# A two-layer decoder on one core: the last stage's units ahead of its later key scores, and the value biases of two stages carried into the output biases

## What is computed

```python
x = x + L0_attn(ln(x))          # random-feature attention, 16 heads of 8, biases on q, k, v, o
x = x + L0_xattn(ln(x), ctx)    # softmax attention over the context, masked by query row, biases
x = x + L0_ffn(ln(x))           # four binary trees that route each row to a leaf of a table
x = x + L1_attn(ln(x))          # causal softmax attention, no biases
x = x + L1_xattn(ln(x), ctx)    # softmax attention over the context, bias on o
x = x + L1_ffn(ln(x))           # product keys: 8 heads, top 16 of 32 x 32 experts
```

```python
v = split_heads(x @ Wv.T + bv)
out = einsum(qf, context, d_inv)        # rows are averages: the weights of a row sum to 1
return out @ Wo.T + bo

sx, ix = top_k(sim[0], 16); sy, iy = top_k(sim[1], 16)     # sim: scores of xn against the keys
scores, pk = top_k(sx[:, None] + sy[None, :], 16)
h = gelu(xn @ table_down[indices].T) * softmax(scores)
out = h @ table_up[indices]
```

## Time and profile before

| | us |
|---|---|
| median of 3 runs | 779.19 (779.06, 779.19, 783.67) |
| the profiled execution | 782.85 |
| its span | 781.1 |
| PE busy | 658.5 (84%) |
| DVE busy | 605.9 (78%) |
| ACT busy | 442.2 (57%) |
| POOL busy | 320.4 (41%) |

### The profile page before, as it was taken

The page is one execution under the profiler, slowest core; times in us unless marked ns, Lnnn a source line. Parts: engine busy times, 40 slices in busy tenths (PEclk is TensorE's granted clock), DMA queues, the critical chain, the costliest instruction groups (busy, mean ns, idle before and its releaser), DMA issues. The chain is left out here.

```text
span 781.1 us, 14578 instructions
## 1 busy us (share of the span) xinstructions
PE 658.5 (84%) x4849; PEld 500.8 (64%) x4849; DVE 605.9 (78%) x2444; ACT 442.2 (57%) x1064; POOL 320.4 (41%) x315
## 2 busy tenths in 40 slices
PE   4969978786888989898788799989879688888898
PEld 2538534443476877786777467655446677787897
DVE  5794686874788989996879777877547689999984
ACT  1333105554565988798977255566545655555562
POOL 4150242821424333231146322221013698888983
PEclk9995558988987999999999999999989899999999
DMA  8000021100786989998652221111000000000000
GB/s 251 3 1 3 12 73 47 43 2 3 297 373 236 422 306 381 340 418 353 224 218 52 61 63 48 48 45 46 2 1 1 1 1 5 4 5 5 4 5 8
DMA packets 38931, 86.07 MB, mean 110 GB/s; under 512 B 3993, under 2 KB 30146, under 8 KB 30664
## 3 DMA queue, kind: packets, MB, share of 16 engines
q0 software_dynamic: 9216, 69.47, 22.6%
q1 hardware_dynamic: 29640, 15.67, 7.6%
HBM read 74.43 MB, written 0.52 MB: 96 GB/s over the span
## 5 line engine op out<-in xcount | busy, mean ns | idle before, releaser
L842 ACT ACTIVATE arena<-arena,hact 128x128 f32<-128x128 f32 x512 | 155.4, 388 | 1.0
L722 ACT ACTIVATE arena<-psum 128x512 f32<-128x512 f32 (+1 forms) x192 | 101.5, 561 | 57.6 <-PE psum L1475 57.1
L617 POOL TENSOR_TENSOR arena<-arena 128x1024 f32<-128x1024 f32 x64 | 121.1, 1911 | 22.6 <-DVE arena L1317 17.0
L1170 DVE CUSTOM_DVE_ANT_0 arena<-arena,fx 128x128 f32<-128x128 f32 x384 | 106.3, 345 | 5.4 <-DMA arena<-tab_q,leaf_no 3.4
L888 ACT ACTIVATE psum<-arena,tneg 128x1024 f32<-128x1024 f32 x64 | 71.5, 1118 | 62.2 <-DVE arena L1317 29.6
L1863 PE MATMUL psum<-arena 128*128 128x128 f32 x688 | 86.7, 283 | 20.3 <-DVE arena L1317 12.9
L976 DVE TENSOR_REDUCE rowmax<-psum 128x2 f32<-128x512 f32 x128 | 81.5, 686 | 24.1 <-PE psum L1457 22.1
L1863 PEld LDWEIGHTS psum<-arena 128*128 128x128 f32 x688 | 82.0, 197 | 23.8 <-DVE arena L1317 15.4
L1754 PE MATMUL psum<-identf,arena 128*128 128x128 f32 x544 | 77.2, 299 | 5.5 <-ACT arena L842 4.4
L1457 PE MATMUL psum<-arena 128*128 128x256 bf16 (+1 forms) x384 | 73.8, 283 | 9.3 <-DVE rowmax L976 8.2
L1754 PE MATMUL psum<-arena,identf 128*128 128x128 f32 x544 | 73.4, 285 | 6.0 <-ACT arena L842 5.4
(11 more groups left out here) (235 smaller groups left out, 1197.0 us busy)
## 6 DMA issues: line engine op xcount, KB each, us to landing
arena<-parts SPq DMA_DIRECT2D x144, 64.0 KB
w_sb<-attn_w SPq DMA_DIRECT2D x1, 768.0 KB, 8.2
x<-x_in SPq DMA_DIRECT2D x1, 512.0 KB, 4.4
fx<-ctx_in SPq DMA_DIRECT2D x1, 512.0 KB, 5.0
picked<-mask_in SPq DMA_DIRECT2D x1, 512.0 KB, 6.1
wq_sb<-peer_wq SPq DMA_DIRECT2D x1, 512.0 KB, 7.9
down_sb<-table_down SPq DMA_DIRECT2D x1, 512.0 KB, 8.9
up_sb<-table_up SPq DMA_DIRECT2D x1, 512.0 KB, 8.8
```

The lines of the kernel that those rows point to most:

```text
L617: nc.gpsimd.tensor_tensor(grid[k % 3].rearrange("p (i j) -> p i j", i=PK), sim[:, t, h, :].unsqueeze(2).to_broadcast([P, PK, PK]), sim[:, ...
L722: nc.scalar.activation(probs[k % (2 * HG)][:, 0:w], bank(2 + k % 2, 0, w), ACT.Exp, scale=float(D) ** -0.5).then_inc(probs_ready, 1)
L842: a = nc.scalar.activation(w, w, ACT.Copy, scale=hact[i % 2][:, l:l + 1])
L1170: i = nc.vector.tensor_tensor_reduce(w, w, src, 1.0, r[:, LW * E + l:LW * E + l + 1], ALU.mult, ALU.add, hid[g % 4][:, l:l + 1])
```

## The change

**In the last stage.** PE no longer does the key scores 4 to 7 ahead of the units of the second half. It does `sims(4)` and `sims(5)` behind the last unit, and `sims(6)` and `sims(7)` behind the mix of heads 0 and 1 of tile 0. ACT copies score 4 ahead of the tile loop and scores 5, 6 and 7 behind the exponentials of heads 1, 2 and 3. Scores 4 to 7 use banks 2 and 3 (`sim_bank`), so PE waits for all of them ahead of tile 1. ACT makes the diagonals of tile 0 in pairs behind the first four exponentials, where it made all behind the second. DVE sums the weights of tile 0 ahead of the first product, where it did so behind it.

```diff
+        def out_bias(a):
+            return psum[0:3, 7 * BANK + P * (a + 1):7 * BANK + P * (a + 2)]
...
+        def sim_bank(t):
+            return bank(t % 2 + t // 4 * 2)
...
@@ POOL @@
+            power(0)
             link(nc.gpsimd.memset(blockm[:, :, :], 1.0))
...
             for n in range(B):
-                power(n)
+                if n:
+                    power(n)
                 squares(n)
...
@@ ACT @@
-            copy(bias_c[:, 4:6], bank(6, 4, 6), columns_ready)
+            copy(bias_c[:, 2:9], bank(6, 2, 9), columns_ready)
...
             def peer():
-                for i in range(2):
-                    if i:
-                        evac_px(i)
-                    for t in range(2 if i == 0 else 4, 4 + 4 * i):
-                        evac_sims(t)
-                    for u in range(B * i, B * i + B):
-                        evac_unit(u)
+                evac_sims(2)
+                evac_sims(3)
+                for u in range(B):
+                    evac_unit(u)
+                evac_px(1)
+                for u in range(B, UNITS):
+                    evac_unit(u)
+                evac_sims(4)
                 act.wait_ge(unit_ready, UNITS)
...
-                        if k == 1:
-                            for i in range(4):
-                                diagonals(0, 2 * i, 2 * i + 2)
+                        if k < 4:
+                            diagonals(0, 2 * k, 2 * k + 2)
+                        if 1 <= k < 4:
+                            evac_sims(4 + k)
...
@@ DVE @@
-            split_bias(nc.vector, link, 2 * P, 4 * P)
-            nc.vector.tensor_copy(bias_w[:, 0:1], bias_p[:, 2 * P:2 * P + 1]).then_inc(bias_ready, 1)
...
+                if 0 < n < B - 1:
+                    o = bias_sb[:, (4 * n - 1) * P:4 * n * P]
+                    link(nc.vector.tensor_tensor(o, out_bias(n - 1), o, ALU.add))
                 link(nc.vector.tensor_copy(sv, half_norm[:, 1, :]))
...
                 if 0 < n < B - 1:
-                    split_bias(nc.vector, link, (4 + 2 * n) * P, min(6 + 2 * n, 9) * P)
+                    o = (4 * n - 1) * P
+                    split_bias(nc.vector, link, o, o + n * P)
...
+                weight_sum(0)
                 for t in range(T):
...
-                        if k == 0:
-                            weight_sum(0)
...
@@ PE @@
-            BIAS = {(0, 2): 2, (0, 3): 3, (1, 2): 6, (1, 3): 7, (3, 3): 8}
+            BIAS = {(0, 3): 3, (1, 3): 7, (3, 3): 8}
...
-            pe.wait_ge(bias_ready, 1)
             pre_v(0)
...
+                if 1 <= n < B - 1:
+                    value_bias(n - 1)
...
+            def value_bias(a):
+                if a == 0:
+                    pe.wait_ge(columns_ready, 1)
+                else:
+                    pe.wait_ge(in_ctx, 48)
+                nc.tensor.matmul(out_bias(a), bias_c[:, 4 * a + 2:4 * a + 3].to_broadcast([P, 3]), w_sb[:, 4 * a + 3, :],
+                                 start=True, stop=True)
...
+                sims(2)
+                sims(3)
+                for u in range(B):
+                    unit(u)
+                turn_px(1)
+                for u in range(B, UNITS):
+                    unit(u)
+                sims(4)
+                sims(5)
                 pe.wait_ge(unit_ready, UNITS)
-                pe.wait_ge(sim_ready, T)
+                pe.wait_ge(sim_ready, 4)
...
                 for t in range(T):
+                    if t == 1:
+                        pe.wait_ge(sim_ready, T)
...
+                        if t == 0 and h in (0, 1):
+                            sims(6 + h)
```

33 lines of the change are left out of this document (13 added, 20 removed).

## The result

The changed kernel took 772.83 us (median of 769.13, 772.49, 773.16 and 773.53) against 779.42 for the kernel before in the same series, a ratio of 0.9893 with a 95% interval of 0.9847 to 0.994. That is 6.6 us, where the forecast was 2.9. Two further series of the changed kernel are among the experiments; the median of all its 15 executions is 771.3.

A forecast was written before the change was run, and what follows sets the result against it. It took as bounds DVE's 5.98 us wait for ACT's first exponential in the last stage, and DVE's nearly unbroken work in the opening. Opening -0.1 and last stage -2.8 took 779.19 to 776.3 us, range 771.5 to 780.9.

The forecast's parts named there:

- Last stage, -2.8: Tile 0: first exponential 2.35 us sooner, DVE's weight sum (0.43) moved into its wait; next choice 2.8 us sooner.
- The beat: Last stage's ring of waits between DVE, POOL and ACT, repeated each tile; claimed to carry 2.8 us to the end.
- rival E: Last stage: the ring's beat, not its start, sets the end; only 0.1 us is left, 779.1; chance 0.03.
- Rival B: Last stage, tile 0: PE at half clock makes tile 7's key score late; 2.1 us lost, 778.4; chance 0.11.
- the place with least room: Last stage, tile 0: the fifth exponential, behind tile 7's key score; claimed hidden with 0.6 us to spare.
- Opening, second pass, +1.34: DVE's second bias split, widened from 128 to 256 columns, its scaling held by POOL's clear; ends 1.34 us later.
- rival A: Opening: the second split pass is not held more than now, giving 1.3 us more, 775.0; chance 0.12.
- Opening, -0.95: PE's features start 0.95 us sooner: 0.65 from the first value projection, 0.3 from the earlier power on POOL.
- In the second stage the missing bias matmuls fall ... nothing: Second stage: they fall behind the projection POOL waits for, or on a PE waiting for DMA; worth nothing.
- Rival D: The half-clock stretch of PE containing 64 to 82 us ends early; 5.6 us won, 770.7; chance 0.12.
- one of my own signs of being wrong: Forecast is wrong if the half-clock stretch in which 64 to 82 us lie has another length.
- Rival C: Slower than before, if the half-clock stretch lasts some 3 us longer in dense work; 780.8; chance 0.10.

The follow-up runs named there:

- e11: Changed kernel plus 24 unread PE products in the gap behind the opening, and POOL's node split waiting for DVE's third five-operation chain: 763.94 us, ratio 0.9793.
- e1: Kernel before with only the last stage's part of the change: 777.17 us, ratio 0.9969.
- e16: Changed kernel as it is, measured again: 771.01 us, ratio 0.9876.
- e13: Changed kernel with PE's gap filled and POOL's node split in two, three operations early and eight behind DVE's third chain: 761.01 us, ratio 0.9767.
- e4: Kernel before with only the value biases carried into the output biases: 772.37 us, ratio 0.9899.
- e9: Changed kernel with POOL's node split waiting until DVE's third chain of five operations is done: 769.93 us, ratio 0.9855.
- e14: Kernel before with PE's gap filled and POOL's node split waiting behind DVE's third chain: 769.96 us, ratio 0.9867.
- e15: Changed kernel with an overwritten 3x128 product put back ahead of each second-stage value product: 775.43 us, ratio 0.9947.
- e8: Kernel before with only the second stage's value bias carried into its output bias: 773.28 us, ratio 0.9916.

## Where the prediction held and where it failed

- **Last stage, -2.8: right in mechanism, 0.3 to 0.9 too large.** Counted from the addition to `x` ahead of the stage (588.66 and 577.90, 10.76 apart), the first exponential is 2.04 sooner (612.96 and 600.16) where I had 2.35. The load starts 0.35 behind POOL's differences (598.65 against 597.90 + 0.40), and I had put it 0.06 behind. With `weight_sum`'s 0.43 this makes 2.48, and the stretch shows 2.5. But only the changed kernel's first profile and e11's have a tile 0 of 58.8; in the seven others with this last stage it takes 59.2 to 59.4, which is 1.9 to 2.1 less than 61.3. The beat carried the head start to the end (131.1 and 130.7), so rival E is out.
- **Rival B's mechanism is the usual case.** In those seven profiles PE does key score 6 at the lower speed (two matmuls 1.91 where they take 1.02, at a granted clock of 0.50 in e1 and e16), and ACT stands idle 2.72 ahead of its copy. In e1:

```profile
610.49 1.91 PE L1835 MATMUL psum<-wq_sb,maskrow 128*128 128x512 f32 x2
```

```profile
612.44 0.60 ACT L663 ACTIVATE arena<-psum 128x512 f32<-128x512 f32 x1 [2.72 <-PE psum L1835]
```

  DVE then waits 0.28 or 0.29 for ACT at the fourth product, so the place with least room lay one head ahead of where I had it, at score 6 and not at score 7. The cost is 0.6 and not 2.1. In the changed kernel's first profile the same idle is 1.54, and nothing is lost.
- **Opening, second pass, +1.34: wrong in the changed kernel's first profile, right in others.** The scaling was not held. It started at 42.54, POOL's clear at 42.75, and it took 0.28; the clear had been 0.13 ahead in my estimate. The pass takes 8.45 against 8.19. That is rival A. I gave it 0.12 although 0.13 us decided it, and behind an opening that had changed by microseconds that margin was worth nothing. Of ten profiles with the new pass seven show 8.45. In the other three it takes 9.5 to 9.6, about what I forecast: in e13 the scaling is held as I had it, in e4 and e9 one cast is held through both clears. The rows of e13 and of e9:

```profile
42.67 3.51 DVE L271 TENSOR_SCALAR bias_p<-arena,identf 3x256 bf16<-3x256 bf16 x1
```

```profile
43.25 6.58 DVE L274 CAST arena<-arena 3x256 bf16<-3x256 f32 x1
```

- **Opening, -0.95: too small, because I moved PE's instructions and left their speed.** The features start 1.39 sooner, and PE reaches full speed at 15.2 us. In e1, whose opening is the old code, it is 19.0 and round 3 starts at 52.32; before's profiled execution (24.1, 54.72) was a late one, as e14's was (54.56). So of the 4.0 us by which round 3 is sooner, some 2.4 are that execution's, and about 1.6 the change's. Over the other profiles of the changed opening the 1.6 scatters: round 3 starts anywhere from 49.85 to 51.76.
- **"In the second stage the missing bias matmuls fall ... nothing": this is the step that failed.** They are eight products, 2.0 us of PE, and they are on the path: in the first pair of profiles the stretches up to the first, the second and the third chain are each 0.5 to 0.9 shorter. The last 0.5 of it, the wait of 1.79 that becomes 1.28, decides how many of the third chain's operations are held. In the place of nothing, this term measured 4.4 us (e15 against e16, 12 and 7 executions), through the third chain and through the clock near 90 us and behind the chain. Nothing in the prediction stood for it, neither a term nor a rival, for I never read 147 to 160 us.
- **Rival D, the half-clock stretch: partly.** In the change it is over for good at 117.6 and not at 123.1, and it is broken from 90.3 to 97.1: 61.5 us at the lower level where it was 68.3. So one of my own signs of being wrong came, another length of this stretch. The 5.6 us that I gave D had no row behind it. The stretch from the first addition to the third unit is 2.0 shorter. It takes 64.8 to 66.2 in the unfilled kernels with the second stage's products and 63.5 to 64.9 in those without, and in e8, with the old opening, it is 64.9 against e1's 66.2, so this too hangs on those products and not on the opening alone. How much of it is the products' own time and how much the clock is not separated.
- **Rival C, a longer half-clock stretch,** did not come.

The forecast of -2.9 was then -2.8 that gave 1.9 to 2.5, and -0.1 that stood for about 1.6 (opening), 2.0 (first addition to third unit) and 2.5 to 4.6 (third unit: 24.1 less 21.6 or 19.5). These add up to 8.0 to 10.7, more than the 6.6 measured at first and about the 7.3 to 10.0 of the later series. They are differences of single profiled executions, so they bear the scatter named above.

Left open: what sets the moment at which PE reaches full speed in the opening (13.3 to 15.2 us in executions of the changed kernel, 18.6 to 24.1 in kernels with the old opening), why the clock comes back near 90 us where the second stage's products are gone, and why the stretch from 220 to 589 us differs by up to 7 us between executions whose code there is the same.

## What to carry to other kernels

Where DVE runs a chain of short operations on the path, look at what POOL does at that time: an operation of 0.2 us becomes one of 2 us, and half a microsecond of shift elsewhere decides between two holds and four. Give POOL's bulk work a wait behind the chain, or split it so that it ends ahead of the next; here that is one line, worth 6.4 us to the kernel before and too little to be sure of (1.4) to the changed one, whose chain is held less. And when work ahead of such a place gets shorter by anything at all, don't cost it at nothing: read the rows behind it for a collision whose order it may turn over.

## What the runs showed of the hardware

- **DVE held by POOL.** On 128x32 a cast took 0.18 free and 2.13 held, a scaling by a constant 0.18 and 1.75, a `tensor_tensor` with both inputs in SBUF 0.19 and 1.76. Row maxima from PSUM took 0.69 on average from 100 to 180 us in every profile looked at, beside POOL's work or not. Casts and scalings, which have one full input, were held beside POOL's clears (3.12 and 3.51 on 3x256) as well as beside its operations that read SBUF. A `tensor_tensor` with two inputs in SBUF was held only by the latter: a subtraction on 3x256 took 0.41 at 46.97, in the middle of a clear, while one on 3x128 took 1.17 at 30.83, beside POOL's square that began at 30.82, where 0.28 is usual. So the 0.28 at 51.05, which I read as speaking against the rule of two inputs, was only the case of the clear. The Trainium skill, SBUF — State Buffer, section Who interferes with whom, says just this: such an instruction contends with a GpSimd instruction that reads SBUF, "not with one that only writes it". The traces agree with it (1.17 and 1.76 beside POOL's reads, 0.41 and 0.28 beside its clears), and with its rule that the later one waits for the whole instruction of the other: held operations end 0.04 to 0.14 us behind POOL's in the rows above.
- **PE's clock after a gap.** Filling one gap of 5.75 us with products that nobody reads gave 5 to 7 us. In its profile the 8 us behind it ran at a granted clock of 1.00, and 0.50 began at 62.2 instead of 49.3.
- **Two sorts of slow PE.** In the opening four features took 3.78 us at a granted clock of 1.00 and 1.96 later at the same 1.00; from 49 us on the slow matmuls go with a granted clock of 0.50. The granted clock doesn't show the first sort.
- **Scatter.** One kernel's executions on one chip lay up to 13 us apart, and profiles of one code show it as a different start of full speed in the opening and as stretches at the lower granted clock. Where a change is worth less, the rows that recur in every profile of one lot and in none of the other (the 7.0 and the 4.5 here) decide more than the medians do.
